# Last pair of heads of a decoder layer: half of the out-projection ahead of the second half's weighing, two token tiles to a PSUM bank

## The reference, cut to what matters

```python
x = x + attn(layernorm(x))            # a state-space scan over 32 heads of 8 channels, state 64, chunks of 128
x = x + 0.6 * sigmoid(si + sj + b) + 0.4 * layernorm(x)   # si, sj from ctx_512
x = x + moe(layernorm(x))             # 7 routed experts, top 2, and a shared one: up, silu gate, down
# inside attn, for each chunk and head:
y_intra = (C @ B.T * decay) @ (x * dt);  states = (B * state_decay).T @ (x * dt)
y_inter = (C * exp(cum)) @ prev;         y = y_intra + y_inter + D * x
out     = (y * silu(z)) @ W_out.T
```

## Time and profile before

| | |
|---|---|
| median of 3 runs | 415.57 us (415.22 to 416.32) |
| the profiled execution, its own time | 417.49 us |
| its span in the trace | 415.8 us |
| PE busy | 392.3 us, 94% of the span |
| DVE busy | 333.7 us, 80% |
| ACT / POOL busy | 227.4 us / 176.8 us |
| mean granted TensorE clock | 0.992 of full |

### The profile page before, as it was taken

One profiled execution on the slowest core, in us unless ns is written; L12 is line 12 of the kernel. 1 busy time (PEld: TensorE's weight loads), 2 busy tenths in 40 slices (PEclk: granted clock), 3 DMA queues, 4 the chain that ended last, 5 costly groups with the idle time before them and its releaser, 6 DMA issues.

```text
span 415.8 us, 8825 instructions
## 1 busy us (share of the span) xinstructions
PE 392.3 (94%) x2989; PEld 289.5 (70%) x2989; DVE 333.7 (80%) x565; ACT 227.4 (55%) x421; POOL 176.8 (43%) x208
## 2 busy tenths in 40 slices
PE   2899999999999999998999999599999999999996
PEld 1677666666667666664666667368897888978886
DVE  3687998999899998998988939819959678596685
ACT  5657455555555555558876631354555545555451
POOL 3699411011110111105546740226575865768561
PEclk9999999999999999999999999889999999999999
DMA  6402211322101221014231150000022020200002
GB/s 185 105 2 56 64 58 10 107 61 61 47 20 55 60 61 57 18 51 135 60 87 44 47 154 9 2 0 2 1 77 56 23 76 0 76 0 2 0 1 102
DMA packets 35932, 21.13 MB, mean 51 GB/s; under 512 B 17048, under 2 KB 33760, under 8 KB 35904
## 3 DMA queue, kind: packets, MB, share of 16 engines
q1 hardware_dynamic: 35904, 20.78, 17.7%
HBM read 18.13 MB, written 1.31 MB: 47 GB/s over the span
## 4 chain that ended last, share of the span: by engine, by line
PE 60%; DVE 18%; ACT 7%; issue 6%; POOL 5%; DMA 1%; DVEq 1%; ACTq 0%; SPq 0%; POOLq 0%
PE bank L1275 21%; PE bank L1468 7%; PE bank L1251 6%; POOL el L652 5%; PE bank L1388 4%; DVE conv L1012 4%; PE bank L1241 4%; DVE xres L1199 4%; PE bank L1456 3%; DVE conv L1220 2%; DVE ewl L1080 2%; PE bank L1261 2%; PE bank L1476 2%; PE bank L1415 2%; PE bank L1244 2%
## 5 line engine op out<-in xcount | busy, mean ns | idle before, releaser
L1012 DVE SCALAR_TENSOR_TENSOR conv<-bank,taps,conv 128x510 f32<-128x510 f32 (+2 forms) x204 | 150.8, 745 | 22.4 <-ACT conv L691 17.5
L1275 PE MATMUL bank<-uth,parts 128*128 128x512 f32 x272 | 96.7, 411 | 2.1 <-DVE utl L995 1.4
L691 ACT ACTIVATE conv<-bank,tap_b,taps 128x512 f32<-128x512 f32 x68 | 52.9, 778 | 57.3 <-PE bank L1275 57.2
L565 POOL TENSOR_TENSOR ce<-conv,ecx 128x512 f32<-128x512 f32 x15 | 19.4, 1295 | 123.1 <-DVE conv L1012 122.7
L1275 PEld LDWEIGHTS bank<-uth,parts 128*128 128x128 f32 x272 | 51.1, 188 | 16.3 <-DVE conv L1012 4.4
L647 POOL TENSOR_TENSOR ul<-conv,uh 128x512 fp32r<-128x512 f32 x32 | 42.9, 1358 | 42.3 <-ACT uh L913 29.3
L652 POOL TENSOR_TENSOR el<-conv,parts 128x512 fp32r<-128x512 f32 x30 | 44.3, 1504 | 30.3 <-ACT parts L925 30.3
L1275 PE MATMUL bank<-utl,parts 128*128 128x512 f32 x136 | 56.4, 415 | 0.0
L1208 DVE CAST uh<-conv 128x512 fp32r<-128x512 f32 x28 | 26.0, 967 | 22.5 <-ACT conv L909 22.3
L1095 DVE SCALAR_TENSOR_TENSOR g<-dec,bank 128x512 f32<-128x512 f32 x64 | 40.9, 679 | 1.7 <-PE bank L1388 1.7
L1220 DVE TENSOR_TENSOR conv<-conv 128x512 f32<-128x512 f32 x32 | 31.4, 1014 | 13.0 <-ACT conv L930 13.0
(11 more groups left out here) (206 smaller groups left out, 732.1 us busy)
## 6 DMA issues: line engine op xcount, KB each, us to landing
w_raw<-in_L_attn_W_in_dram SPq DMA_DIRECT2D x17, 256.0 KB, 3.2
ecx<-ecum_dram SPq DMA_DIRECT2D x32, 128.0 KB, 2.9
ew_raw<-in_L_ffn_Wup_dram SPq DMA_DIRECT2D x7, 256.0 KB, 3.3
ew_raw<-in_L_ffn_Wgate_dram SPq DMA_DIRECT2D x7, 256.0 KB, 3.3
ew_raw<-in_L_ffn_Wdown_dram SPq DMA_DIRECT2D x7, 256.0 KB, 3.6
xres<-in_x_dram SPq DMA_DIRECT2D x2, 512.0 KB, 4.1
out_dram<-xres SPq DMA_DIRECT2D x4, 256.0 KB, 2.2
yi<-yev SPq DMA_DIRECT2D x56, 16.0 KB, 1.8
```

The lines of the kernel that those rows point to most:

```text
L691: act.activation(conv[q][:, j, HALF * h:HALF * (h + 1)], bank[u % 2][:], ACT.Identity, bias=tap_b[q][:, j:j + 1], scale=taps[q][:, j, TAPS ...
L1012: dve.scalar_tensor_tensor(out=dst[:, :, d:SEQ], in0=src[:, :, 0:SEQ - d], scalar=taps[q][:, j, TAPS - 1 - d:TAPS - d], in1=dst[:, :, d:SE ...
L1275: ins = pe.matmul(bank[u % 2][:], w, x_t, start=(i == 0), stop=(i == 3 * KD - 1))
```

## The change

Eight things are altered, all around the last pair:

1. PE's order in `last_pair`. Tiles 0 and 1 are projected out (`project_out`, without the late pairs) right behind `turn_b`, tiles 2 and 3 behind `weigh(n, q, 1)`. The exponents 2 and 3 and `b_dot_c` of the second half come behind them.
2. Two token tiles share a PSUM bank (`o_tile`), and the late pairs are added tile by tile (`late_parts`, order 0, 2, 1, 3), with waits between tiles of one bank, instead of all four tiles in turn.
3. `load_late(1)` is issued right behind `load_late(0)`, ahead of `place_y(14)` and of `load_ecx(16)`.
4. DVE runs `gate_last(0)` between the first two and the last two products `g`.
5. ACT normalises four tiles of the first half and two of the second; DVE none and two (before: ACT two and none, DVE two and four).
6. DVE takes the moments and roots of the second half ahead of `rest_turned` 4 and 5.
7. `keep_warm` ahead of `turn_tokens(4, ..)` has 15 matmuls instead of 9.
8. In expert 0 the first tile of `gate` stands ahead of `turn_tokens` 6 and 7, the second behind them.

```diff
         def o_tile(t):
-            return bank[(2, 3, 4, 5, 0, 1, 6, 7)[t]][:, 0:DM]
+            return bank[(0, 4)[t // 4] + t % 4 // 2][:, DM * (t % 2):DM * (t % 2 + 1)]
...
                     sp.wait_ge(misc_read, 2)
                     load_late(0)
+                    load_late(1)
                 if 1 < n < PAIRS:
                     sp.wait_ge(y_read, n - 1)
                     place_y(n - 1, 1 - q, yev_out[1 - q])
...
-                if n == PAIRS - 1:
-                    load_late(1)
...
-            normalise(T, range(2), 3)
-            split_turned(4, 4)
-            split_turned(5, 5)
+            normalise(T, range(4), 2)
             root(slice(4, 8), 4)
+            split_turned(4, 6)
+            split_turned(5, 7)
...
+                    if u == 1 and isinstance(n, int) and n == PAIRS:
+                        gate_last(0)
...
-                if isinstance(n, int) and n == PAIRS:
-                    gate_last(0)
...
-            normalise(T + 2, range(2, 4))
             moments(4, range(4, 8), from_projection, mv_done)
-            rest_turned(4, 4)
-            rest_turned(5, 5)
             inverse_roots(slice(4, 8), 4, None, False)
+            rest_turned(4, 6)
+            rest_turned(5, 7)
             second_block(range(4, 8))
             moments(T + 4, range(4, 8), from_residual, mv_done)
             inverse_roots(slice(T + 4, 2 * T), 5)
-            normalise(T + 4, range(4, 8))
+            normalise(T + 4, range(4, 6))
...
             def last_pair(n, k, q):
+                def project_out(tiles):
+                    for t in tiles:
+                        residual(t)
+                        for k in range(KD):
+                            onto_o(k, t)
+                def late_parts(tiles):
+                    for i, t in enumerate((tiles[0], tiles[2], tiles[1], tiles[3])):
+                        if i >= 2:
+                            pe.wait_ge(o_done, tiles[0] + i - 1)
+                        for p in range(2):
+                            late_onto_o(p, t)
                 exponents(n, k, q, 0)
                 exponents(n, k, q, 1)
                 b_dot_c(n, q, 0)
                 weigh(n - 1, 1 - q, 3)
                 turn_b(n, q)
+                project_out((0, 1))
+                weigh(n, q, 0)
+                new_state(n, q)
                 exponents(n, k, q, 2)
                 exponents(n, k, q, 3)
+                turn_state(n)
                 b_dot_c(n, q, 1)
-                new_state(n, q)
-                weigh(n, q, 0)
-                turn_state(n)
                 from_state(n, 0)
                 weigh(n, q, 1)
-                for t in range(4):
-                    residual(t)
-                for k in range(KD):
-                    for t in range(4):
-                        onto_o(k, t)
-                for p in range(2):
-                    for t in range(4):
-                        late_onto_o(p, t)
+                project_out((2, 3))
+                late_parts(range(4))
                 weigh(n, q, 2)
                 from_state(n, 1)
                 weigh(n, q, 3)
-                for t in (4, 5, 7, 6):
-                    residual(t)
-                    onto_o(0, t)
-                    onto_o(1, t)
-                for p in range(2):
-                    for t in range(4, 8):
-                        late_onto_o(p, t)
+                project_out(range(4, 8))
+                late_parts(range(4, 8))
...
-            pe.wait_ge(o_read, 1)
-            keep_warm(2, up_weights, 9)
-            turn_tokens(4, 4)
-            turn_tokens(5, 5)
+            keep_warm(2, up_weights, 15)
+            turn_tokens(4, 6)
+            turn_tokens(5, 7)
...
                     logits(0)
+                    gate(0, 0, range(1))
                     turn_tokens(6, 6)
                     turn_tokens(7, 7)
-                    gate(0, 0, range(2))
-                    pe.wait_ge(lgT_read, 1)
+                    gate(0, 0, range(1, 2))
                     up(0, 0, range(2, 4))
```

More of the change, by code:

```diff
@@ L899, in expert @@
                 for v in range(4):
-                    if first and v == 1:
+                    if first and v == 2:
                         root(slice(T + 4, 2 * T), 5)
-                    if first and v == 2:
+                        normalise(T + 6, range(6, 8), 3)
                         copy_logits(0)
@@ L1093, in body @@
                     at_least(dve, y_done, a - 1)
-                    dve.scalar_tensor_tensor(out=g[b][:], in0=dec[b][:], scalar=1.0, in1=cb_bank(n, u // 2, b)[:],
+                    dve.scalar_tensor_tensor(out=g[b][:], in0=dec[b][:], scalar=1.0, in1=bank[2 + b][:],
                                              op0=ALU.min, op1=ALU.mult).then_inc(g_done, 1)
@@ L1104, in body @@
                         split_router()
-                if isinstance(n, int) and n == PAIRS:
-                    gate_last(0)
             over_pairs(dve, body)
             def from_projection(t):
-                dve.wait_ge(o_done, t + 1)
+                dve.wait_ge(o_done, t - t % 4 + 3 + t % 4 // 2)
                 return o_tile(t)
@@ L1420, in residual @@
             def residual(t):
-                if t < 2:
-                    pe.wait_ge(g_done, 4 * (PAIRS - 1) + t + 1)
-                elif t < 4:
-                    pe.wait_ge(exp_done, 4 * (PAIRS - 1) + t + 1)
-                elif t < 6:
-                    pe.wait_ge(g_done, 4 * (PAIRS - 1) + t - 1)
-                else:
-                    pe.wait_ge(y_read, PAIRS + 7 - t)
-                pe.matmul(o_tile(t), ident[:], xres[:, t, :], start=True, stop=False)
+                if t < 4:
+                    pe.wait_ge(tap_done, 12 * PAIRS + 9 + 3 * (t // 2))
+                else:
+                    pe.wait_ge(exp_done, 4 * (PAIRS - 1) + t // 2 + 1)
+                pe.matmul(o_tile(t), ident[:], xres[:, t, :], start=(t % 2 == 0), stop=False)
             def onto_o(k, t):
@@ L1444, in late_onto_o @@
                 ins = pe.matmul(o_tile(t), yev[1 - p][r, P * (t // 4):P * (t // 4 + 1)], wsp[r, p, :],
-                                start=False, stop=(p == 1))
+                                start=False, stop=(p == 1 and t % 2 == 1))
                 if p == 1:
@@ L1462, in b_dot_c @@
                 pe.wait_ge(tap_done, 12 * n + (9, 12)[h])
-                at_least(pe, g_done, 4 * (n - 1) + (0 if isinstance(n, int) and n == PAIRS else 2 * h))
+                at_least(pe, g_done, 4 * (n - 1) + 2 * h)
                 for i in range(4):
@@ L1467, in b_dot_c @@
                         r = slice(NS * j, NS * (j + 1))
[L1468 removed]
+                        ins = pe.matmul(bank[2 + j][:, i * P:(i + 1) * P], conv[q][r, 0, s], conv[q][r, 1, s],
                                         start=True, stop=True)
@@ L1625, in logits @@
                 s = slice(HALF * i, HALF * (i + 1))
-                three(bank[(4, 0)[i]][0:NE, :], lambda k: [(wrh[:, k, :], uth[:, k, s]), (wrh[:, k, :], utl[:, k, s]),
+                three(bank[i][0:NE, :], lambda k: [(wrh[:, k, :], uth[:, k, s]), (wrh[:, k, :], utl[:, k, s]),
                                                        (wrl[:, k, :], uth[:, k, s])], KD).then_inc(lg_done, 1)
```

15 lines of the change are left out of this document (6 added, 9 removed).

## The result

The changed kernel takes 421.42 us (median of 4 runs, 421.06 to 424.29) against 415.53 us for the kernel before on the same chip (4 runs): a ratio of 1.0152, interval 1.0118 to 1.0187. I had forecast 418.2 with a range to 420.3. The direction was right, the size was less than half of what came, and the range missed it. Executions in a slower state of the chip (739.03 us of e3, 419.56 and 484.23 of e7, 544.94 of the kernel before beside e5 to e8) are left out of all medians and ratios.

A forecast was written before the change was run, and what follows sets the result against it. PE, busy in 94% of the span, was taken as the bound outside its few stops. 8.15 us lost by the first turn, less 2.0 and 3.5 won back, gave +2.6: 418.2 us, range 415.0 to 420.3.

The forecast's parts named there:

- SP's queue: `load_late(1)` ahead delays `place_y(14)` by 7.7 us; POOL starts on `yi` at 241.5, its queue moving with it.
- the slow pace: Four `place_y` issues taken at 3.29 us; at the quick 2.57 us all would come 0.7 us sooner.
- The sum: Change in total time: 8.15 - 2.0 - 3.5 = +2.6 us on the median 415.57, giving 418.2 us.
- PE to the first turn: PE waits for `yi`, then longer late parts and `keep_warm`; first turn at 267.1 against 258.95, 8.15 us lost.
- the fall of the clock: Rival: clock falls in PE's new 4.3 us stop, half clock for 4.3 us behind it; +1.6, 419.8 us, chance 0.24.
- The late parts: Each set of 16-row late matmuls on PE, issued tile by tile, takes 2.65 us instead of 1.08.
- From the first turn to the second: DVE's earlier roots and only two tiles to normalise put the second turn at 275.7; 2.0 us won back.
- From the second turn to `up`: One gate tile fills the stop and the clock stays up; 2.2 us instead of 5.73, about 3.5 won back.
- The base: Forecast put on the median of the runs, 415.57 us, since the profiled execution's 417.49 lies 1.9 above it.
- no stop: Rival: first half of `yi` is gated in time, so PE does not stop in `project_out`; -2.0, 413.6 us, chance 0.09.
- the fall case: Rival: clock falls in the new stop within the first `project_out`; 419.8 us, chance 0.24.

The follow-up runs named there:

- e3: Kernel before with only `load_late(1)` moved ahead of `place_y(14)`: 427.20 us, ratio 1.0257.
- e7: The edits of e5 and e6 together, with 12 unread `keep_warm` matmuls instead of 15: 416.08 us, ratio 0.9987.
- e5: Changed kernel with `load_late(1)` put back and `var` formed by `scalar_tensor_tensor` instead of `tensor_scalar`: 415.21 us, ratio 0.9987.
- e8: Kernel before with only the gates' part: one gate tile ahead of the second turn, one behind, ScalarE's root one place later: 412.99 us, ratio 0.991.
- e2: Changed kernel with `load_late(1)` put back behind `load_ecx(16)`, nothing else: 415.16 us, ratio 0.9988.
- e4: Changed kernel with 17 unread matmuls in PE's new stop, between `onto_o(0, 0)` and `onto_o(1, 0)`: 420.6 us, ratio 1.011.
- e10: Kernel before with POOL's second `ul` made to wait for DVE's last `xn`: 413.72 us, ratio 0.9951.
- e9: Kernel before with the late matmuls issued tile by tile, tiles still in four banks: 415.57 us, ratio 0.9995.
- e6: e2 with the last half's late parts written two tiles at a time, taking turns between two banks: 415.48 us, ratio 0.9999.
- e1: Kernel before, unchanged, timed and profiled once more: 415.77 us, ratio 1.0001.
- e11: e8 with ScalarE normalising two of the last four tiles and 5 unread matmuls in the stop before the second turn: 411.0 us, ratio 0.9887.
- e12: e11 without the 5 unread matmuls in the stop before the second turn: 411.95 us, ratio 0.9914.

## Why the prediction was wrong

**SP's queue, right.** POOL was to start 2.5 us behind the first `residual` and started 2.28 behind it. The choice of the slow pace was wrong, though: the four issues of `yi` took 2.51, and one issue of 1.16 stood at 228.63 in `load_late(1)`. An issue of 1.1 to 1.7 us stands at about this time in e3 too (1.62 at 228.87), and in e2 the four `yi` issues, which start at 228.21, take 3.38. In all fourteen profiles one such issue starts between 227 and 230 us, whichever DMA it is. So it seems to belong to the moment and not to the DMA; what makes it is open. The sum came out the same.

**PE to the first turn: the failed step.** "Against it: ahead of that stop PE ran matmuls with only 8 weight columns, here it runs full ones." This made me leave the fall of the clock as a rival, at 0.24. It fell, at 0.68 on average over the last 2.5 us of the stop, and stood at 0.50 over the whole of the 4.4 us that followed. The sum had nothing for it, and the rival 1.6; it cost 2.2 (e4 against the changed kernel, and +2.3 in the table). From `onto_o(1, 0)` to `weigh` it took 3.71 us for 1.93 in e4, the 1.8 that the rival had. From `weigh` to `b_dot_c` it took 2.00 for 1.37, 0.6 where I had a few tenths; `b_dot_c` itself took its 1.16 again. And under 0.2 of it hid behind `ce`, the wait that e4 has there and the changed kernel has not (both halves of `ce` were ready by 247.8). The rule of the Trainium skill (TensorE: Matmul & The Clock Gate, HAM oscillation — how this bites in real kernels), that each long enough wait puts the clock back, agrees with this trace at the new stop of 3.90 us, as it did before at the one of 4.67; my reason for setting it aside was a guess without a row behind it. The length of a stop alone does not settle it here: with a second stop of 1.51 us the clock stayed up in the changed kernel and in e2 and fell in e4 and e5, and with one of 3.61 us (e10) it stayed up in 4 of 9 runs.

**The late parts: right price, wrong reason.** I took 2.65 a set for the reason that a tile's two matmuls read the same 16 rows one behind the other, and that only the last record of one tile can run beside the next tile. It measured 2.33 to 2.39. e9 issues them in just this order and needs 1.17, so the order costs nothing. Here are the two halves of the first set of the changed kernel, tiles 0 and 2 and then tiles 1 and 3 (PE's timeline, asked for each half by itself):

```profile
252.82 1.14 PE L1433 MATMUL bank<-wsp,yev 16*128 16x256 f32 x8
254.01 1.21 PE L1433 MATMUL bank<-wsp,yev 16*128 16x256 f32 x8
```

Each half, two tiles, is as long as the whole set of four tiles in e9, and the second begins when the first has ended. So two tiles beside each other cost as much as four. What doubles the price is the program's own wait for `o_done` between the tiles of one bank, which lets only two tiles run at a time. e6 keeps such a wait and has 1.13 and 1.20 us for its halves. The Trainium skill (TensorEngine Tiling (Array Packing), Gotcha 1: PSUM Pressure) says that matmuls on different rows cannot access one bank at the same time, and that the program has to see to it. No run here puts the tiles of a set in one bank without the wait, so whether it could be left out stays open.

**From the first turn to the second: mis-sized.** "From L1123 to the first normalised tile it is 4.75 us": it measured 5.59 (269.75 to 275.34). The moved roots do bring DVE's chain forward by 0.8 us (`var` begins 6.14 us behind the turn, in e1 and e8 6.97). But there it meets POOL's `ul` and waits 1.0 us. So what the moved roots won went straight into a wait. The wait itself was in the trace that I read, one row further on: the 2.44 us for four `xn` in the earlier trace rows held 1.06 of it, as e10 shows, and I halved them to 1.22 without asking what they were made of. That number came out right (275.34 to 276.60) only because ACT's two tiles take 1.09 us; DVE's take 0.73.

**From the second turn to `up`, right.** 2.34 us for a forecast 2.2, at a clock of 1.00. There was some luck in it: I had argued from the stop being short, and in e4, with the same stop of 1.51 us, the clock did fall here and the turn took 1.97 us.

**The base.** Against e1, with the same tail behind `up`, the changed kernel is 5.84 us slower (421.06 and 415.22): 5.27 from the first `b_dot_c` of the last pair to `up` (43.12 and 37.85) and 0.6 ahead of it. Of these 0.6 I can say nothing: in the two profiles of the kernel before, that `b_dot_c` starts at 236.98 and at 235.20. Of the forecast's miss of 3.2 us, then, 2.3 are in the table above, 0.45 is the longer fall in the trace that I took as base, and the rest is this spread.

The case "no stop" had 413.6 us; e2, which is that case, has 415.2. In its profiled execution, at a clock of 1.00, it is 34.61 us from the first `residual` to `up` (238.00 to 272.61), for 34.3 in that case; the six of its twelve runs at such a clock have a median of 414.1, the others took 415.6 to 419.2. So most of these 1.6 us are falls of the clock in some of the runs, and that the fall case misses by 1.6 too (419.8 for 421.4) is chance.

## What to carry to other kernels

Before a DMA is put ahead of another in an in-order queue, write down who waits for the later one and how long it has been early; here 7.7 us of issue went ahead of the transfers of `yi` and `ecx`. `ce`, which follows them, had been only 1.4 us early (240.97 for 242.41), and the new order asks for `yi` sooner. It cost 6 to 11 us. Where a new stop of PE is about as long as one at which the trace shows the clock fall, count the work behind it at half clock, and try to fill what is left of a stop with unread matmuls (e4, e11) if a bank is free. When the price of an instruction comes from a row, look first at what the other engines did during that row: 2.44 us for four `xn` was 1.38 of work and a wait.

## What the runs showed of the hardware

DVE and POOL shut each other out here. While POOL's `tensor_tensor` `ul` (two inputs in SBUF) runs, a `tensor_scalar` or a `scalar_tensor_tensor` of DVE from SBUF does not end until it does: 1.19, 1.20 and 1.20 us in place of 0.17 for 4 columns in the changed kernel, e5 and e6, 2.44 in place of 1.38 for four tiles in e1. The statistics do not wait: in the changed kernel `stats` of four tiles takes 1.40 us at 271.52, beside `ul`, and 1.40 at 260.29, where POOL is idle. The Trainium skill (SBUF — State Buffer, Who interferes with whom) has this as its rule: GpSimd and VectorE share a pair of ports as an exclusive lock, which VectorE can take with a `tensor_scalar`, in the modes that use both of its ports, and with an instruction that has two inputs in SBUF. All these rows agree with it; in which mode a `tensor_scalar` ran, no row shows.

The clock can fall while PE is busy. In e4 it went to half within a row of 15 `keep_warm` matmuls (5.30 us in place of 3.74) that followed the 16-row late parts, and PE had been busy for 3.16 of the 3.20 us ahead of it. In e6 it fell behind the first late parts (two `onto_o` matmuls at 249.20 take 1.91 us in place of 1.03). The profiled executions of e1, e8 and e9, whose late parts are half as long, show no fall in that place, but those of the changed kernel, e2 and e5, with the long ones, show none either. So what brings it on stays open.

One fall costs about 2 us in this kernel: runs of e12 at 0.995 and at 1.00 lie 1.9 us apart (413.5 against a mean of 411.6).
